# Both layer normalisations of an attention layer moved from VectorE and GpSimd to ScalarE, and VectorE's bank emptying moved ahead of the diagonal's bias

## The reference

```python
x = x + attn(layernorm(x))      # rotary q and k, ALiBi bias, softmax, projection with bias
x = x + (h @ W.T + b + (h @ V_r) @ C.T)     # h = layernorm(x)

def _layernorm(x, axis=-1, eps=1e-05):
    m = jnp.mean(x, axis=axis, keepdims=True)
    v = jnp.var(x, axis=axis, keepdims=True)
    return (x - m) / jnp.sqrt(v + eps)
```

## Time and profile before

| | |
|---|---|
| median of 3 runs | 2271.48 us (2270.88 to 2272.22) |
| the profiled execution | 2274.01 us, span 2272.7 us |
| PE busy | 94% (matmul rows; their ends are modelled) |
| DVE busy | 87% |
| ACT busy | 61% |
| POOL busy | 51% |
| mean granted clock of PE | 0.978 of full speed, full in all slices of the middle |

### The profile page before, as it was taken

How to read it: one execution, slowest core, us unless ns; L and a number is a source line. 1 busy time by engine, 2 the same in 40 slices (tenths; PEclk the granted TensorE clock), 3 DMA queues, 4 the chain that set the end, 5 groups by cost and what they waited for, 6 DMA issues and landing times. The chain is left out here.

```text
span 2272.7 us, 77397 instructions
## 1 busy us (share of the span) xinstructions
PE 2140.8 (94%) x31524; PEld 1130.2 (50%) x31524; DVE 1980.0 (87%) x5949; ACT 1383.4 (61%) x1666; POOL 1151.2 (51%) x966
## 2 busy tenths in 40 slices
PE   3899999999999999999999999999999999999996
PEld 1245555555555555555545555555555555555553
DVE  5599999999998989999989999998999999999972
ACT  0166666666666666666666666666666666666662
POOL 3436555554545545555555455555545555554421
PEclk8699999999999999999999999999999999999997
DMA  5323433333333332343333333333333333323310
GB/s 117 110 77 87 117 84 106 110 85 99 105 107 87 105 108 77 105 115 87 102 111 85 99 105 110 86 107 114 85 100 105 108 87 106 115 79 104 97 32 24
DMA packets 158868, 218.49 MB, mean 96 GB/s; under 512 B 19024, under 2 KB 104912, under 8 KB 158512
## 3 DMA queue, kind: packets, MB, share of 16 engines
q1 hardware_dynamic: 157232, 211.44, 32.9%
q10 hardware_dynamic: 1280, 2.10, 0.3%
HBM read 36.52 MB, written 16.78 MB: 23 GB/s over the span
## 5 line engine op out<-in xcount | busy, mean ns | idle before, releaser
L529 DVE CUSTOM_DVE_ANT_0 junk<-ps_s,alibi 128x512 bf16<-128x512 f32 x2048 | 1323.5, 683 | 191.7 <-PE ps_s L364 155.3
L673 ACT ACTIVATE pt<-ps_t 128x1024 f32<-128x1024 f32 x1024 | 1050.8, 1026 | 606.1 <-DVE ps_t L539 601.0
L364 PE MATMUL ps_s<-at 64*128 64x512 f32 x2048 | 817.5, 462 | 20.6 <-DVE row_max L529 9.7
L372 PE MATMUL ps_t<-at 64*128 64x512 f32 x2048 | 776.3, 453 | 1.2 <-ACT pt L673 1.2
L385 PE MATMUL ps_o<-pt,v_one 128*17 128x128 f32 x16384 | 642.5, 275 | 2.9
L385 PEld LDWEIGHTS ps_o<-pt,v_one 128*17 128x17 f32 x16384 | 424.0, 98 | 328.3 <-issue 220.7
L539 DVE SCALAR_TENSOR_TENSOR ps_t<-diag,slope,ps_t 128x256 f32<-128x256 f32 x1024 | 495.4, 484 | 27.6 <-PE ps_t L372 27.6
L364 PEld LDWEIGHTS ps_s<-at 64*128 64x128 f32 x2048 | 331.4, 186 | 294.2 <-DVE row_max L529 215.3
L802 POOL TENSOR_TENSOR rope_a<-rope_a,swapped 128x512 f32<-128x512 f32 x128 | 161.6, 1284 | 469.5 <-DMA swapped<-rope_b 469.5
L372 PEld LDWEIGHTS ps_t<-at 64*128 64x128 f32 x2048 | 326.4, 185 | 33.2 <-ACT pt L673 26.0
L335 PE MATMUL ps_misc<-xt,wqkv_t 128*32 128x512 f32 x2048 | 279.6, 620 | 13.8 <-DVE x L563 6.0
(11 more groups left out here) (72 smaller groups left out, 1447.8 us busy)
## 6 DMA issues: line engine op xcount, KB each, us to landing
at<-halves SPq DMA_DIRECT2D x192, 512.0 KB, 5.1
swapped<-rope_b SPq DMA_DIRECT2D x256, 128.0 KB, 2.6
x_in<-in_L_attn_x_dram SPq DMA_DIRECT2D x32, 512.0 KB, 3.9
num<-o_sb SPq DMA_DIRECT2D x512, 32.0 KB, 2.0
x_res<-in_L_attn_x_dram SPq DMA_DIRECT2D x32, 512.0 KB, 4.2
out_dram<-x_hat SPq DMA_DIRECT2D x32, 512.0 KB, 5.9
at<-spread_den SPq DMA_DIRECT2D x60, 64.0 KB
at<-max_t ACTq DMA_DIRECT2D x128, 16.0 KB
```

The source lines that it names most:

```text
L364: pe.matmul(ps_s[:, t % 2, :], operand(n, 0)[:, t * P:(t + 1) * P], operand(n, 1), start=True, stop=True).then_inc(s_done, 1)
L372: pe.matmul(ps_t[:, j, :], operand(n, 1)[:, j * P:(j + 1) * P], operand(n, 0), start=True, stop=True).then_inc(t_done, 1)
L529: dve.tensor_tensor_reduce(junk[:, t % 2, :], ps_s[:, t % 2, :], alibi[:, off:off + N], 1.0, LOWEST, ALU.add, ALU.max, row_max[:, hb % 2, ...
L673: act.activation(pt[:, h % 2, 2 * pair:2 * pair + 2, :], ps_t[:, 2 * pair:2 * pair + 2, :], ACT.Exp).then_inc(exp_done, 1)
```

## The change

- VectorE no longer takes statistics. ScalarE does both normalisations, a tile of 128 tokens x 256 channels at a time: `take_mean` (an ACTIVATE with the scale -1/256 whose accumulator is the negative mean), `take_squares` (Square with the negative mean as bias, its accumulator the sum of squares), and `normalise` (scale and bias of each token). That is 12 ACTIVATEs for each normalisation. The elementwise outputs of the first two go to the target tile and are overwritten.
- GpSimd keeps three small operations on 128x4 (`deviation`): add epsilon, power, and minus the mean times the result. The factor sqrt(256) that is left over is applied when the transposes are copied out (`copy_turned`).
- The two transposes to `xt` are now both in slot 1 (before: slots 0 and 1).
- VectorE's `divide` and `add_linear` stand ahead of `diagonal_bias` in a half. PE spreads the denominators ahead of `weighted_values`. The output is stored one slot earlier, ahead of the loads of slot 11 that follow in SP's queue.

```diff
-            def ln_stats(b, src, ln, bn, tokens): ...
-            def ln_mean_var(b, ln, bn, aggr): ...
@@ vector_program, one half of a slot
                         row_maximum(n, 2 * half + 1)
-                    if nt is not None:
-                        diagonal_bias(nt, half)
                     b = batch_at(slot, 31)
                     if b is not None:
                         divide(b, half)
...
+                    if nt is not None:
+                        diagonal_bias(nt, half)
                     b = batch_at(slot, 30)
@@ scalar_program
+            def take_mean(b, t, src, dst, ln, means):
+                act.activation(dst[:, t, :], src[:, t, :], ACT.Copy, scale=-1.0 / C,
+                               accum_out=minus_mean[:, ln, t:t + 1]).then_inc(means, 1)
+            def take_squares(b, t, src, dst, ln, means, done):
+                act.wait_ge(means, T * b + t + 1)
+                act.activation(dst[:, t, :], src[:, t, :], ACT.Square, bias=minus_mean[:, ln, t:t + 1],
+                               accum_out=squares[:, ln, t:t + 1]).then_inc(done, 1)
+            def normalise(b, t, src, dst, ln, shifts, done):
+                act.wait_ge(shifts, b + 1)
+                ins = act.activation(dst[:, t, :], src[:, t, :], ACT.Identity, bias=shift[:, ln, t:t + 1],
+                                     scale=rstd[:, ln, t:t + 1])
@@ second normalisation, ahead of exponentials(nt, 0)
+                b = batch_at(slot, 35)
+                if b is not None:
+                    mean2(b, 0)
+                    mean2(b, 1)
+                b = batch_at(slot, 36)
+                if b is not None:
+                    mean2(b, 2)
+                    mean2(b, 3)
+                b = batch_at(slot, 37)
+                if b is not None:
+                    normalise2(b, 0)
+                    normalise2(b, 1)
@@ and ahead of exponentials(nt, 1), behind the copy of raw
+                b = batch_at(slot, 35)
+                if b is not None:
+                    squares2(b, 0)
+                    squares2(b, 1)
+                b = batch_at(slot, 36)
+                if b is not None:
+                    squares2(b, 2)
+                    squares2(b, 3)
+                b = batch_at(slot, 37)
+                if b is not None:
+                    normalise2(b, 2)
+                    normalise2(b, 3)
@@ pool_program
+            def deviation(b, ln, ready, veps, rs, done):
+                pool.wait_ge(ready, T * (b + 1))
+                pool.tensor_tensor(var_eps[:, ln, :], squares[:, ln, :], eps[:, :], ALU.add).then_inc(veps, 1)
+                pool.wait_ge(veps, b + 1)
+                pool.tensor_tensor(rstd[:, ln, :], var_eps[:, ln, :], minus_half[:, :], ALU.pow).then_inc(rs, 1)
+                pool.wait_ge(rs, b + 1)
+                pool.tensor_tensor(shift[:, ln, :], minus_mean[:, ln, :], rstd[:, ln, :], ALU.mult).then_inc(done, 1)
...
-                b = batch_at(slot, 36)
-                if b is not None:
-                    inverse_deviation(b, 1, aggr_done2, veps_done2, rstd_done2)
-                    normalise(b, x1, x_hat2, 1, rstd_done2, centred2, xhat_done2)
+                b = batch_at(slot, 37)
+                if b is not None:
+                    deviation(b, 1, squares_done2, veps_done2, rstd_done2, shift_done2)
```

More of the change, by code:

```diff
@@ L21 @@
 MAX_BIAS = 8.0
+ROOT_C = float(C) ** 0.5
 SCALE = float(D) ** -0.5
@@ L463, in tensor_program @@
                         project_qk(cc, half, bank)
[L464 to L467, removed]
+                    b = batch_at(slot, -15)
+                    if b is not None:
+                        turn_tokens("xt", b, half, x_hat, xhat_done, b + 1, xt_done)
                     b = batch_at(slot, 38)
@@ L472, in tensor_program @@
                         max_rows(hb)
+                    b = batch_at(slot, 31)
+                    if b is not None:
+                        spread_denominators(b, half)
                     if nv is not None:
@@ L624, in vector_program @@
                             add_linear("proj", b, u, x1, x_res, res_biased, x1_done)
[L625 to L630, removed]
                         b = batch_at(slot, 41 + u)
@@ L674, in exponentials @@
                                ACT.Exp).then_inc(exp_done, 1)
+            for t in range(T):
+                mean1(0, t)
+            for t in range(T):
+                squares1(0, t)
+            for t in range(T):
+                normalise1(0, t)
             act.wait_ge(weights_turned, 1)
@@ L680, in scalar_program @@
                 nt = head_at(slot, T_LAG)
[L681 to L684, removed]
-                bx = batch_at(slot, 38)
-                if bx is not None:
-                    act.wait_ge(xhat_done, min(bx + 4, NB))
-                    copy_turned("x2t", bx, 0, x2t, x2t_done)
+                b = batch_at(slot, -19)
+                if b:
+                    mean1(b, 0)
+                    mean1(b, 1)
+                b = batch_at(slot, -18)
+                if b:
+                    squares1(b, 1)
+                    mean1(b, 2)
+                b = batch_at(slot, -17)
+                if b:
+                    squares1(b, 2)
+                    squares1(b, 3)
+                b = batch_at(slot, -16)
+                if b:
+                    normalise1(b, 2)
+                    normalise1(b, 3)
+                bx = batch_at(slot, -15)
+                if bx is not None:
+                    copy_turned("xt", bx, 0, xt, xt_done)
+                b = batch_at(slot, 35)
[10 more added lines that the diff above has]
+                    normalise2(b, 1)
+                b2 = batch_at(slot, 38)
+                if b2 is not None:
+                    copy_turned("x2t", b2, 0, x2t, x2t_done)
                 if nt is not None:
@@ L720, in scalar_program @@
                     exponentials(nt, 1)
+                hb = half_at(slot, 8)
                 if hb is not None:
@@ L870, in sync_program @@
                     place_fourth_rows()
-                b = batch_at(slot, 44)
+                b = batch_at(slot, 43)
                 if b is not None:
```

103 lines of the change are left out of this document (49 added, 54 removed).

## The result

The changed kernel takes **2389.78 us** (median of 4 runs, 2384.84 to 2396.61), against 2271.18 (2270.58 to 2272.22) for the kernel before: ratio 1.0524 with an interval of 1.0494 to 1.0553. It is 118.6 us slower. Slower was forecast, but by 42 us (2313, range 2245 to 2350), so the time lies outside the range. The profiled execution took 2392.73 us, its span is 2391.4, and the mean granted clock of PE fell from 0.978 to 0.946.

A forecast was written before the change was run, and what follows sets the result against it. PE alone was taken to set 4.20 us slots, VectorE slots 1 and 5. +1.7 (slots 3 to 6) - 0.38 - 0.48 (slots 2, 10, 11) + 0.5 = +1.34 a batch, +42 us: 2313, range 2245 to 2350.

The forecast's parts named there:

- The prices of ScalarE's passes: ScalarE's normalisation passes: 0.39 us for a mean, 0.48 for a square or a normalising pass.
- Slots 3 and 4: Second normalisation's means and first squares: slot 4 ends at 9.15 instead of 8.91, the two slots lose 0.24 us.
- The stand of 0.5 us: Start of slot 4: slot 3's first exponential ends at 4.65, PE wants it at 4.20, so PE stands for 0.5 us.
- Slots 10 and 11: Bank emptied ahead of the diagonal, so both slots fall to 4.20 us: -0.48 a batch together.
- slot 2: Counted with what VectorE and the bank order give back: 4.58 to 4.20 us, -0.38 a batch.
- Slots 5 and 6: Work in series delays slot 5's first exponential; PE goes on 4.95 us into slot 5 instead of 3.49.
- that is 1.45 more: Slot 6's matmul, issued 1.45 us later into slot 5 than before, counted as that much loss a batch.
- Slots 13 to 1: First normalisation: sum between -0.3 and +0.9 us a batch, taken as +0.5.
- Slot 1: With both transposes and two copies through one bank: from 3.23 to about 3.7 us, +0.5.
- Slot 14: Reciprocals still wait for the denominators' DMA: gains 0.1 us, or 0.46 if the DMA is early.
- Slot 15: PE meets the denominators' lateness directly and `o_sb` is copied only behind the last product: 0 to +0.35 us.
- It does what it says: Rival, chance 0.27: faster, ScalarE's 24 ACTIVATEs fall into its waits; 2202 us, or 2237 to 2260 with half.
- Worse than that: Rival, chance 0.10: upper prices, +0.9 in slots 13 to 1, no gain in slot 2; +2.5 a batch, 2350 us.

The follow-up runs named there:

- bank order alone: The kernel before with only VectorE's `divide` and both kinds of `add_linear` put ahead of `diagonal_bias`, statistics staying on VectorE: 2256.83 us, ratio 0.9934.
- one power: The kernel before with one unused GpSimd power more in the second normalisation, other engines' instructions unchanged: 2332.88 us, ratio 1.0267.

## Why the prediction was right about the direction and wrong about the time

**The prices of ScalarE's passes: right.** Groups of the changed kernel (line, operation, shapes, count, busy us, mean ns):

```profile
L631 ACT ACTIVATE x_hat<-x,minus_mean 128x256 f32<-128x256 f32 x128 | 63.7, 502 | 0.0
...
L626 ACT ACTIVATE x_hat<-x 128x256 f32<-128x256 f32 x128 | 52.2, 415 | 13.5 <-DVE x L552 13.5
...
L626 ACT ACTIVATION_READ_ACCUMULATOR x_hat<-x 128x1 f32 x128 | 25.1, 196 | 0.0
```

The rows overlap, so the price is the spacing. Two means start 0.41 apart (987.94 and 988.35) where 0.39 was taken, two squares 0.50 (994.47 and 994.97), two normalising passes have a row of 0.59 each in 1.09 together, thus 0.50, where 0.48 was taken. One term of the 0.39, the 0.03 for a source in SBUF, rests on no row (and 0.27, 0.08 and 0.03 make 0.38); the sum doesn't hang on it. As an estimate from the figures of the Trainium skill, "ScalarE: Activation LUTs", section "What ACT_TABLE_LOAD costs", an ACTIVATE of 256 elements takes 0.40, 0.49 and 0.59 us with no, one and two per-partition pointers. This case's rows agree (0.415, 0.502, 0.59). As an estimate from the same section of the Trainium skill, two means would start 0.31 apart. 0.41 was measured; the accumulator's read-out, which follows each mean as a row of 0.19 to 0.20, is the likely difference, though no run here has a mean without it.

**Slots 3 and 4: right.** 9.15 us were forecast together, 9.16 are the mean. The stand of 0.5 us at the start of slot 4 is there too, but as a late start and not as a wait of the listing, since PE's score matmul has a row over the same time. The exponential ends at 989.76, and the matmul behind it comes 0.51 us into the slot that starts at 989.30:

```profile
988.75 1.01 ACT L685 ACTIVATE pt<-ps_t 128x1024 f32<-128x1024 f32 x1
...
989.81 0.49 PE L375 MATMUL ps_t<-at 64*128 64x512 f32 x1
```

**Slots 10 and 11: right, slot 2 by luck.** -0.86 forecast for the three, -0.84 measured. The bank order alone confirms 10 and 11. It leaves slot 2 at 4.54, so the forecast -0.38 there came out for another reason than the one given: it is the other side of the +0.52 in slot 1.

**Slots 5 and 6: the chain was right, its consequence wrong.** The copy of `raw`, squares, GpSimd (0.78 waited by ScalarE, 0.7 forecast), two tiles and the exponential bring PE's matmul to 5.01 us, forecast 4.95. In two details it differs: PE waits for the last exponential of slot 4 in slot 5 as well (0.35 us), and 1.06 in slot 6 where 1.5 was named, so the two together are about what was forecast. The failed step is "that is 1.45 more": it carries a delay of one matmul to the end of slot 6 as if PE then went on as before. It didn't: PE ran at half speed, and slots 5 and 6 cost +3.07. With the clock held up by the useless matmuls they cost +1.39, which is the 1.45 of the forecast. The term that the sum puts at nothing, without a word on it, is the clock: 3.07 - 1.39 = 1.68 a batch, 52 us in 31.

**Slots 13 to 1: mis-sized.** +0.5 was taken, in bounds of -0.3 and +0.9; +1.19 was measured, 21 us more in 31 batches. Slot 1 came as forecast (3.75, forecast 3.7). Slot 14 didn't gain (4.75 in both), since VectorE's wait for the denominators' DMA went from 9.5 us in 12 times to 37.7 in 29, as was said. Slot 15 took +0.79 where at most +0.35 was allowed. The forecast counted only PE's lateness behind the denominators there (0.42 a batch in the mean). It left out that VectorE's second division moves into slot 15 with them (put back, slot 15 is at 4.63): VectorE is busy for 4.91 of 5.16 us in the mean, where it was 4.37 of 4.37, and PE waits another 0.50 a batch there for row maxima. PE's new wait for the copy of `o_sb` wasn't foreseen as one of PE either, but lies in slot 0 (0.49 at 1047.06). I had slot 0 down as losing what it gained by having no transposes, and it did about that (-0.12).

Together: 42 forecast + 50 (slots 5 and 6 beyond the forecast) + 21 + 4 (slot 7, still at half speed) = 117 us, of 118.6.

**The rivals.** "It does what it says" was to decide by slot 5's first exponential: by 2.42 us into the slot it would have been faster. It began at 998.25, 3.96 us in. The busy shares speak as that rival had them, VectorE from 87% to 79%, and the kernel is 5% slower. The Trainium skill, "Perfetto Trace Analysis", section "Identifying the Most-Contended Engine", has the engine of highest occupancy optimized first; among the three beside PE that was VectorE, and by this rule alone one would have taken the wrong side here. "Worse than that" had the right side, but not for its reasons: the prices weren't the upper ones and slot 2 did gain. It lacked the same term. Since all costs were held in engine time at full clock, no bound of my range could reach 2390.

**Left open.** Why the clock fell in every batch of the changed kernel that has a second normalisation, but only in 16 of 29 with one power, where PE stood longer at once (1.41 against 1.06): the changed kernel's PE stands in slot 5 as well (its rows fill 3.01 of 3.46 us), but I ran nothing that varies the two stands apart. Why slots 15 and 0 are still +0.58 a batch with the denominators' spreading put back is only argued (the copy of `o_sb` behind ScalarE's squares and tiles), not shown by a run without it; and how the +1.19 of slots 15, 0 and 1 divides between PE's order and the first normalisation isn't separated by any run.

## What to carry to other kernels

Before moving work to an idle engine that executes in order, write down the chain that the next matmul hangs on, across all engines, and see where in the slot it ends; the free share of the engine says nothing about that. Then price a stand of PE twice: once as its length, and once for the matmuls that follow it, which can come at half speed. And take a bundled change apart: here the bank order alone was worth 15 us, which the whole change hid under a loss of 118, and with a split of GpSimd's last pass, which wasn't in the change, 29.

## What the runs showed of the hardware that I had not expected

- PE's clock fell to its lower level after stands of only 1.06 and 1.41 us (in the changed kernel with another of 0.35 us in the slot before it), with PE busy for most of the time on both sides: 32 stretches and 150 us in 30 batches of the changed kernel, 16 and 68 us with one power more, none with the stand of 0.42 us of the kernel before. With one power the four transposes right behind the stand were still at full speed (0.63) and the matmul after them wasn't (0.67); in the changed kernel the clock was down by the time the stand ended (0.79).
- Two useless matmuls in each batch (the wider takes 1.12 us) made the changed kernel 52 us faster by filling those stands.
- ScalarE's accumulator read-out is an instruction of its own with a row of 0.19 to 0.20 us, over twice VectorE's 0.08.
